# Four graph-attention layers, 32 batches: weights staged all at once, loading over four engines, and orders of their own for the first and last batches

## The chip, the cores and the metric

One core of a Trainium2 chip (trn2). The metric is device time of one execution in microseconds (us), the median of three runs. Every output is float32.

## The reference, cut to what matters

`x` is 32 batches of 512 nodes with 256 features, `adj` a 512 x 512 matrix of integers shared by all batches. Four layers follow one another, each of the form `x = x + layer(relu(layernorm(x)))`:

```python
def attention(h, mask, W, a, slope):          # one head
    Wh = h @ W
    e = leaky_relu((Wh @ a1)[:, None] + (Wh @ a2)[None, :], slope)
    return softmax(where(mask, e, -inf), axis=-1) @ Wh

# layer 0: four heads of 64 features, mask adj != 0, elu
# layer 1: out = relu(h @ mlp1_w + mlp1_b)                     256 -> 512
#          out = elu(elu(attention(out, none, W_fc))) + out    512 features, no mask
#          out = relu(out @ mlp2_w + mlp2_b)                   512 -> 256
#          out = relu(elu(elu(attention(out, adj > 0, W_hand))) + out)
# layer 2: mask (adj > 0) or the diagonal, elu
# layer 3: mask adj != 0, relu
```

## The kernel before, in words

**Arithmetic.** Projections and MLPs are done in three passes on split numbers (`mm3`, L397): each operand has a rounded part "hi" and the rest "lo", and hi x hi, hi x lo, lo x hi are summed. So each of the seven weights (W0, WM1, WFC, WM2, WHA, W2, W3) is held as hi and lo, and each weight of an attention layer has extra columns with its product with `a`. An attention layer transposes normalised x on TensorE (`turn`, L406), makes hi (ScalarE) and lo (VectorE), projects (`project`), takes scores, spreads a row of them over the partitions with transposes (`row`, L440), makes the weights P of 128 x 512 on VectorE from that row and the mask (`weigh`, L646), and multiplies by P (`attend`, L450, 257 columns; layer 0 at L489, 65 columns per head; the unmasked one of layer 1 at L526). The first MLP's result is split into hi on ScalarE (L917) and lo on GpSimd (L1031).

**Lanes.** Batch b runs in lane b % 3, which has its own SBUF buffers (`R`, `Z`, `hT`, `hws`, `rowt` ...) and its own ring of two or three of the eight PSUM banks; x has four slots. Batches in different lanes overlap, two of the same lane don't.

**Order.** `tensor_batch`, `vector_batch`, `scalar_batch` and `pool_batch` are generators: each writes out one batch's instructions for one engine and yields after every step (112 steps on TensorE, 154 on VectorE, 108 on ScalarE, 8 on GpSimd). `in_turns` (L82) lays them out by a string `TURNS` (L66) for each engine. In period t, digit c takes one step of batch t - c, and "w" one step of the loading. The same string serves all 35 periods; digits of batches that don't exist do nothing. So TensorE's 27 steps with digit 0 are layer 0 of the youngest batch, the 51 with digit 1 the wide part of layer 1 and the begin of its second attention, the 34 with digit 2 the rest.

**Loading.** SyncE (SP) fetches x0, x1, x2, then each weight into the same pair of buffers `halves` (parts of lane 2's `R`), one after another (`sync_loads`, L242): it waits for the last weight's subtraction (`s_wlo`) and transposes (`s_wT`). ScalarE makes hi (L319), VectorE lo (L295); for a weight with `a`, TensorE transposes each block of 128 rows (L338), VectorE copies the result (L304), TensorE multiplies by `a` (L345), VectorE writes the extra columns (L307, L309). W0 is loaded ahead of everything, then adj, in two halves, into the same buffers: VectorE makes the 0/1 rows (L358), TensorE transposes them (L392), VectorE copies them into masks of bytes in sixteen pieces (L367). The other weights are loaded by the "w" steps. Batches 1 and 2 wait ahead of their first normalisation on VectorE until all of it is done:

```python
            if b in (1, 2):
                w.wait_ge(s_wAl, 24)
                w.wait_ge(s_wlo, K_BEFORE[7])
                w.wait_ge(s_wT, 12)
                w.wait_ge(s_mT, 16)
```

Of the kernel before, what the change touches and what calls it, by code (L numbers as in the profile page):

```python
# [64 lines left out]

TURNS = {  # L66
    "pe": (
        "ww22112111100w11www1w1w01011220022www0ww22121021w121122w2120121w20w01110ww1ww1102www210102020w20w11w"
        "0w20120101121w10w20w001101w1w211122w212w121121w1"),
    "dve": (  # L70
        "ww2w1w22111w122w21www102w2wwww0002w22ww2w2w22w0ww02w121w222w21w2210ww10w21www2w00022022ww00210022222"
        "001ww0211w221w10w1112ww2221w110w1221w1200211w1w0110w20w0w1121w11212210w120000011w122w00w22w0001w02w1"
        "w022w111122222"),
    "act": (
        "222211221211122212001211010122100121211220w12212221w222121111w1111122101112ww1122112102121122011w210"
        "11211211211122"),
    "pool": (
        "11w1w1w1222"),
}

def in_turns(batch, turns, loading):  # L82
    going, loads = {}, loading()
    for t in range(B + LANES):
        for c in turns:
            if c == "w":
                next(loads, None)
                continue
            b = t - int(c)
            if 0 <= b < B:  # L90
                if b not in going:
                    going[b] = batch(b)
                next(going[b], None)
    for left in [loads] + list(going.values()):
        for _ in left:
            pass
# [14 lines left out]
def build(nc, x_d, adj_d, L0_W, L0_a, m1_w, m1_b, m2_w, m2_b, fc_w, fc_a, ha_w, ha_a, L2_W, L2_a, L3_W, L3_a, out_d):  # L111
    ctx = ExitStack()
    with ctx:
# [18 lines left out]
        def weights(name, kb, fo, nq):  # L132
# [42 lines left out]
        s_zero, s_const, s_id, s_bias = (new_sem(n) for n in ("zero", "const", "ident", "bias"))  # L175
        s_wl = [new_sem(f"wl{c}") for c in range(2)]
        s_al, s_az, s_whi, s_wlo, s_wT, s_wTe, s_wA, s_wAl = (new_sem(n) for n in (
            "al", "az", "whi", "wlo", "wT", "wTe", "wA", "wAl"))
        s_mrow, s_mT, s_mTe, s_mask = (new_sem(n) for n in ("mrow", "mT", "mTe", "mask"))
# [23 lines left out]
        def freed(b, name, i=0):  # L203

            ring = RINGS[b % LANES]
            n = b // LANES * len(USES) + USE_AT[name, i] - len(ring)
            if n < 0:
                return (s_wAl, 24) if b % LANES == 2 else (s_id, 1)
            _, _, kind, k = USES[n % len(USES)]
            return at(kind, n // len(USES) * LANES + b % LANES, *k)  # L210
# [6 lines left out]
        halves = [R[2][:, 0:2, :], R[2][:, 2:4, :]]  # L217
        wT = Z[1][:, 0:512]
        a_st = Z[1][:, 1056:1088].rearrange("p (k q) -> p k q", q=8)
        id_st = Z[2][:, 0:128]  # L220
        mrow = {"ne": R[1][:, 0:2, :], "gt": R[1][:, 2:4, :]}

        LOADS = [(W0, L0_W, "heads", (0,)), (WM1, m1_w, None, (0,)), (WFC, fc_w, fc_a, (0, 1)), (WM2, m2_w, None, (0,)),
                 (WHA, ha_w, ha_a, (0,)), (W2, L2_W, L2_a, (0,)), (W3, L3_W, L3_a, (0,))]
        KB = [w["kb"] for w, _, _, _ in LOADS]

        K_BEFORE = [sum(KB[:n]) for n in range(8)]
        QK_BEFORE = [sum(w["kb"] for w, _, a, _ in LOADS[:n] if a is not None) for n in range(8)]
        Q_BEFORE = [sum(1 for _, _, a, _ in LOADS[:n] if a is not None) for n in range(8)]
        AL_BEFORE = [sum(8 if isinstance(a, str) else 2 for _, _, a, _ in LOADS[:n] if a is not None) for n in range(8)]  # L230

        def wl_count(n, c):
            return sum(1 for _, _, _, cs in LOADS[:n + 1] if c in cs) + (1 if n > 0 else 0)

        def stage(n):

            w, _, _, cs = LOADS[n]
            per = 1024 // w["fo"]
            return [halves[k // per].rearrange("p a n -> p (a n)")[:, k % per * w["fo"]:(k % per + 1) * w["fo"]]
                    for k in range(w["kb"])]  # L240

        def sync_loads(e, w):  # L242
            for n, (wt, w_d, a_d, cs) in enumerate(LOADS):
                fo, kb = wt["fo"], wt["kb"]
                per = 1024 // fo
                wv = w_d.rearrange("(k p) n -> p k n", p=128)
                for c in cs:
                    k0, k1 = c * per, min(kb, (c + 1) * per)
                    if n == 0:
                        w.wait_ge(s_id, 1)  # L250
                    elif n == 1:
                        w.wait_ge(s_mT, 16)
                    else:
                        w.wait_ge(s_wlo, K_BEFORE[n])
                        w.wait_ge(s_wT, QK_BEFORE[n])
                    dst = halves[c].rearrange("p a n -> p (a n)")[:, 0:(k1 - k0) * fo].rearrange("p (k n) -> p k n", n=fo)
                    e.dma_start(dst, wv[:, k0:k1, :]).then_inc(s_wl[c], 16)
                if a_d is not None:
                    w.wait_ge(s_az, Q_BEFORE[n] + 1)
                    if isinstance(a_d, str):  # L260
                        for h in range(4):
                            for t in range(2):
                                p0 = (h % 2) * 64
                                e.dma_start(a_st[p0:p0 + 64, h // 2, t * 4 + h:t * 4 + h + 1],
                                            L0_a[h, t * 64:(t + 1) * 64].rearrange("(p o) -> p o", o=1),
                                            allow_slow_non_contiguous=True).then_inc(s_al, 16)
                    else:
                        ob = fo // 128
                        for t in range(2):
                            e.dma_start(a_st[:, 0:ob, t],  # L270
                                        a_d[t * ob * 128:(t + 1) * ob * 128, 0].rearrange("(k p) -> p k", p=128),
                                        allow_slow_non_contiguous=True).then_inc(s_al, 16)
                if n == 0:
                    for half in range(2):
                        if half == 0:
                            w.wait_ge(s_wlo, 2)
                            w.wait_ge(s_wT, 2)
                        e.dma_start(halves[half].bitcast(I32), adj_v[:, 2 * half:2 * half + 2, :]).then_inc(s_wl[half], 16)
                    e.dma_start(b1[:, :], m1_b.rearrange("(k p) -> p k", p=128),
                                allow_slow_non_contiguous=True).then_inc(s_bias, 16)  # L280
                    e.dma_start(b2[:, :], m2_b.rearrange("(k p) -> p k", p=128),
                                allow_slow_non_contiguous=True).then_inc(s_bias, 16)

        def vector_load(e, w, n):
            wt, _, a_d, cs = LOADS[n]
            tiles, kb, fo, nq = stage(n), wt["kb"], wt["fo"], wt["nq"]
            if a_d is not None:
                if n:
                    w.wait_ge(s_wA, QK_BEFORE[n])
# [849 lines left out]
```

## Time and profile before

| what | value |
|---|---|
| median of three runs | 3269.46 us (3267.59 to 3269.56) |
| profiled execution | 3268.22 us, span 3266.4 us |
| TensorE (PE) busy | 3148.4 us, 96% |
| VectorE (DVE) busy | 2689.4 us, 82% |
| ScalarE (ACT) busy | 1864.1 us, 57% |
| GpSimd (POOL) busy | 326.2 us, 10% |
| mean granted clock of TensorE | 0.982 |

### The profile page before, as it was taken

To read this page: it belongs to the slowest core of one execution; us is meant where nothing else is said; L and a number is where in the kernel's file an instruction comes from. 1 tells how busy PE (TensorE), PEld (TensorE's weight loads), DVE (VectorE), ACT (ScalarE), POOL (GpSimd) and SP (SyncE) were. 2 spreads that over 40 slices of the span, in tenths; PEclk is the share of its full clock that TensorE was granted. 3 is DMA by queue.
4 is the path that set the end of the run, shared out by engine and by line. 5 is a ranking of instruction groups with operands and counts; after the bars stand their busy time and mean duration, and the time that the engine had idled before them with its cause. 6 is when DMAs were issued, how large, how long until landed. Compare 5 with 4: busy or idle time off the path is not lost.

```text
span 3266.4 us, 55502 instructions
## 1 busy us (share of the span) xinstructions
PE 3148.4 (96%) x20480; PEld 2860.2 (88%) x20480; DVE 2689.4 (82%) x7611; ACT 1864.1 (57%) x4627; POOL 326.2 (10%) x265
## 2 busy tenths in 40 slices
PE   5899999999999999999999999999999999999996
PEld 4888899889889888889988889988989988989985
DVE  5578888888888888888888888888888888888865
ACT  1355556565655565655565655655655655655653
POOL 0011100111100111110111110111110111110010
PEclk7799999999999999999999999999999999999997
DMA  2000000000000000000000000000000000000000
GB/s 65 14 1 14 14 14 1 14 14 14 14 14 1 14 14 14 14 14 1 14 14 14 14 14 3 12 14 14 14 14 8 7 14 14 14 14 7 1 7 13
DMA packets 16332, 41.32 MB, mean 13 GB/s; under 512 B 5312, under 2 KB 6848, under 8 KB 16064
## 3 DMA queue, kind: packets, MB, share of 16 engines
q1 hardware_dynamic: 16064, 37.77, 3.3%
q8 instruction: 165, 2.70, 0.3%
q14 instruction: 103, 0.84, 0.1%
HBM read 20.99 MB, written 16.78 MB: 12 GB/s over the span
## 4 chain that ended last, share of the span: by engine, by line
PE 88%; POOL 4%; ACT 4%; DVE 2%; issue 1%; DMA 1%; SPq 0%; POOLq 0%; ACTq 0%; DVEq 0%
PE bank L399 30%; PE bank L457 20%; PE bank L526 14%; PE bank L489 14%; POOL oTlo L1031 4%; PE bank L445 3%; PE bank L413 3%; PE bank L538 2%; ACT O L915 1%; ACT oThi L917 1%; PE bank L435 1%; PE bank L563 1%; ACT Z L978 0%; PE bank L345 0%; DVE x L846 0%
## 5 line engine op out<-in xcount | busy, mean ns | idle before, releaser
L457 PE MATMUL bank<-hw,R 128*128 128x257 f32 x3072 | 735.9, 383 | 6.2 <-ACT Z L983 3.2
L457 PEld LDWEIGHTS bank<-hw,R 128*128 128x128 f32 x3072 | 566.9, 190 | 108.1 <-issue 24.6
L489 PEld LDWEIGHTS bank<-hw,R 128*128 128x128 f32 x4096 | 515.5, 196 | 17.1 <-issue 7.4
L489 PE MATMUL bank<-hw,R 128*128 128x65 f32 x4096 | 515.0, 274 | 7.3 <-DVE R L653 7.3
L526 PE MATMUL bank<-hw,R 128*128 128x257 f32 (+1 forms) x2048 | 492.9, 380 | 0.0
L653 DVE SCALAR_TENSOR_TENSOR R<-bank,E,mask_ne 128x512 f32<-128x512 f32 x640 | 452.6, 742 | 1.4 <-PE bank L445 1.2
L1024 POOL TENSOR_TENSOR rs<-ve,mhalf 128x4 f32<-128x4 f32 x128 | 145.8, 1139 | 2683.0 <-DVE ve L600 2683.0
L526 PEld LDWEIGHTS bank<-hw,R 128*128 128x128 f32 x2048 | 372.6, 189 | 46.1
L399 PE MATMUL bank<-wfc_hi,oThi 128*128 128x256 f32 (+1 forms) x1024 | 303.3, 296 | 30.6 <-POOL oTlo L1031 29.4
L874 ACT COPY Z<-bank 128x258 f32<-128x258 f32 (+1 forms) x640 | 239.0, 374 | 161.6 <-PE bank L399 157.4
L399 PE MATMUL bank<-wfc_lo,oThi 128*128 128x256 f32 (+1 forms) x1024 | 289.4, 283 | 0.0
L399 PE MATMUL bank<-wfc_hi,oTlo 128*128 128x256 f32 (+1 forms) x1024 | 288.1, 281 | 0.0
L888 ACT ACTIVATE hw<-Z,hw 128x256 f32<-128x256 f32 x512 | 241.9, 504 | 2.1
L399 PEld LDWEIGHTS bank<-wfc_hi,oThi 128*128 128x128 f32 x1024 | 193.7, 189 | 43.8 <-POOL oTlo L1031 43.8
L593 DVE BATCH_NORM_STATS2 st<-x 128x6 f32<-128x256 f32 x512 | 215.8, 422 | 9.9
L945 ACT ACTIVATE Z<-bank,rD 128x256 f32<-128x256 f32 x256 | 121.2, 474 | 160.6 <-PE bank L526 134.3
L1031 POOL TENSOR_TENSOR oTlo<-O,oThi 128x512 fp32r<-128x512 f32 x128 | 179.6, 1423 | 228.3 <-ACT oThi L917 225.7
L399 PEld LDWEIGHTS bank<-wfc_hi,oTlo 128*128 128x128 f32 x1024 | 194.3, 190 | 0.0
L399 PEld LDWEIGHTS bank<-wfc_lo,oThi 128*128 128x128 f32 x1024 | 194.0, 189 | 0.0
L621 DVE TENSOR_SCALAR Z<-x,mv,rs 128x256 f32<-128x256 f32 x512 | 178.2, 407 | 6.7 <-POOL rs L1024 3.4
L1001 ACT ACTIVATE Z<-bank,rD 128x256 f32<-128x256 f32 x128 | 60.6, 473 | 213.0 <-DVE rD L662 213.0
L413 PE MATMUL bank<-identr,Z 128*128 128x128 f32 x1024 | 148.4, 281 | 17.1 <-DVE Z L621 17.1
(199 smaller groups left out, 6828.4 us busy)
## 6 DMA issues: line engine op xcount, KB each, us to landing
x<-in_x_dram SPq DMA_DIRECT2D x32, 512.0 KB, 3.2
out_dram<-x SPq DMA_DIRECT2D x32, 512.0 KB, 2.6
R<-in_adj_dram SPq DMA_DIRECT2D x2, 512.0 KB, 4.5
R<-in_L_gnn_mlp_w_dram SPq DMA_DIRECT2D x2, 512.0 KB, 3.9
R<-in_L_gnn_W_fc_dram SPq DMA_DIRECT2D x2, 512.0 KB, 4.2
R<-in_L_gnn_W_dram SPq DMA_DIRECT2D x3, 256.0 KB, 4.0
R<-in_L_gnn_W_hand_dram SPq DMA_DIRECT2D x1, 256.0 KB, 2.6
Z<-in_L_gnn_a_dram SPq DMA_DIRECT2D x8, 0.2 KB, 3.5
```

Of the source, the lines that this page charges most:

```text
L399: i = e.matmul(out, u, v, start=first and q == 0, stop=last and q == 2, skip_group_check=not group)
L413: i = e.transpose(bk[:, n * 128:(n + 1) * 128], hn[:, n, k * 128:(k + 1) * 128], ident[:, :])
L457: ins = e.matmul(bk[:, 0:257], P[:, j, i * 128:(i + 1) * 128], hw[:, j, 0:257], start=(j == 0), stop=(j == NBLK - 1))
L489: ins = e.matmul(bk[:, i * 66:i * 66 + 65], P[:, (4 * h + j) % PTILES, i * 128:(i + 1) * 128], hv[:, j, h, 0:65], start=(j == 0 and i == 0 ...
L526: ins = e.matmul(bank_of(b, "attf", q)[:, 0:n], P[:, j, i * 128:(i + 1) * 128], hw[:, j, c0:c0 + n], start=(j == 0), stop=(j == NBLK - 1))
L593: e.bn_stats(m["st"][:, n, :], xs[b % XSLOTS][:, n, :]).then_inc(up("stat", b))
L621: e.tensor_scalar(hn[:, n, :], x[:, n, :], m["mv"][:, n, 0:1], m["rs"][:, n:n + 1], ALU.subtract, ALU.mult).then_inc(up("hn", b))
L653: e.scalar_tensor_tensor(P[:, t, :], bank_of(b, "row", p)[:, :], m["E"][:, 1, h, j:j + 1], mask[:, j, :], ALU.max, ALU.mult).then_inc(up(" ...
L874: e.copy(raw[s][:, i, 0:n], bank_of(b, f"h{l}", i)[:, 0:n]).then_inc(up("raw", b))
L888: e.activation(hw[:, n, 0:256], raw[s][:, n, 0:256], ACT.Copy, scale=hw[:, n, 256:257]).then_inc(up("hw", b))
L1024: e.tensor_tensor(m["rs"][:, :], m["ve"][:, :], mhalf[:, :], ALU.pow).then_inc(up("rs", b))
L1031: e.tensor_tensor(oT["lo"][:, fo, :], O1[:, fo, :], f32(oT["hi"][:, fo, :]), ALU.subtract).then_inc(up("o1lo", b))
```

## The change

`TURNS` now has three strings for each engine and one set for SP: one for batches 0 to 2 up to the point where batch 3 starts, with the "w" of the loading in it, one cycle for periods 3 to 27, and one for the last batches, in which digit c is batch 31 - c. SP's stores and loads of x are steps too (`sync_batch`). The cycle has the same numbers of steps as before, in another order; TensorE's begins

```
before, "w" left out: 2211211110011110101122002202212102112112221201212001110111022101...
after:                2211211110011110011122002202212112111201212110221212011010012020...
```

In TensorE's last string batch 30's last step has 8 steps behind it (36 in the old layout), and batch 31 begins layer 1 with 132 steps left in all (117). The new string of TensorE for the start begins

```
wwww00ww00000000w00000001000001w000w00w1w111www00w1w0000ww0000w11000101...
```

Every weight has a buffer of its own that later lanes or slots don't need yet:

```diff
-        halves = [R[2][:, 0:2, :], R[2][:, 2:4, :]]
-        wT = Z[1][:, 0:512]
-        mrow = {"ne": R[1][:, 0:2, :], "gt": R[1][:, 2:4, :]}
...
+        x3 = xs[3].rearrange("p b f -> p (b f)")
+        id_st, wT, a_flat = x3[:, 512:640], rowt[1], x3[:, 640:676]
+        adj_st = R[0][:, 0:4, :].bitcast(I32)
+        mrow = {"ne": R[1][:, 0:4, :], "gt": R[2][:, 0:4, :]}
+        tiles0 = [R[1][:, 4, :], Z[2][:, 0:1024], hws[2].rearrange("p b n -> p (b n)")[:, 0:2048], Z[2][:, 1056:2080],
+                  R[2][:, 4, :], rowt[2], x3[:, 0:512]]
...
+        GROUPS = [(0, (0, 1))] + [(2, (k,)) for k in range(4)] + [(n, (0, 1)) for n in (4, 5, 6)]
```

SP issues all of it without a wait but one (for the zeros that `a` of W0 is written into):

```diff
         def sync_loads(e, w):
...
+            e.dma_start(xs[0][:, :, :], x_v[0]).then_inc(xin[0], 16)
+            load_weights(e, 0)
+            for half in range(2):
+                e.dma_start(adj_st[:, 2 * half:2 * half + 2, :], adj_v[:, 2 * half:2 * half + 2, :]).then_inc(s_adj[half], 16)
+            load_scores(e, w, 0)
+            e.dma_start(xs[1][:, :, :], x_v[1]).then_inc(xin[1], 16)
+            load_weights(e, 1)
...
+            load_weights(e, 2)
+            load_scores(e, w, 2)
+            e.dma_start(xs[2][:, :, :], x_v[2]).then_inc(xin[2], 16)
+            load_weights(e, 3)
+            for n in (4, 5, 6):
+                load_weights(e, n)
+                load_scores(e, w, n)
```

The loading is spread: ScalarE makes hi, copies the transposed weights and two of each mask's four blocks (now 128 x 512 at a time); VectorE does the other two, the 0/1 rows, the extra columns and W0's lo; GpSimd makes every other lo:

```diff
+        def gpsimd_lo(e, w, n):
+            wt = LOADS[n][0]
+            for k in range(wt["kb"]):
+                w.wait_ge(s_whi, K_BEFORE[n] + k + 1)
+                e.tensor_tensor(wt["lo"][:, k, 0:wt["fo"]], staged[n][:, k, :], f32(wt["hi"][:, k, 0:wt["fo"]]),
+                                ALU.subtract).then_inc(s_wlo)
+                yield
+
+        def gpsimd_loads(e, w):
+            yield from power(e, w, 0, 0)
+            yield from gpsimd_lo(e, w, 1)
+            yield from power(e, w, 1, 0)
+            yield from gpsimd_lo(e, w, 2)
+            yield from power(e, w, 2, 0)
+            for n in range(3, 7):
+                yield from gpsimd_lo(e, w, n)
```

The wait of batches 1 and 2 for everything is replaced by waits for the buffer that each place overwrites:

```diff
-            if b in (1, 2):
-                w.wait_ge(s_wAl, 24)
-                w.wait_ge(s_wlo, K_BEFORE[7])
-                w.wait_ge(s_wT, 12)
-                w.wait_ge(s_mT, 16)
+            if b == 2:
+                w.wait_ge(s_whi, K_BEFORE[4])
+                w.wait_ge(s_wlo, K_BEFORE[4] - 2)
...
+            if b == 0:
+                w.wait_ge(s_mrow, 4)
+            elif b == 1:
+                w.wait_ge(s_mT, 4)
+                w.wait_ge(s_empty, 1)
+                w.wait_ge(s_wlo0, 2)
+                w.wait_ge(s_wT, 1)
```

and the load of x3 waits for the weights staged in its slot:

```diff
+        def sync_batch(e, w, b):
+            n = b + LANES
+            if n < B:
+                if n >= XSLOTS:
+                    w.wait_ge(xout[n % XSLOTS], 16 * (n // XSLOTS))
+                else:
+                    w.wait_ge(s_id, 1)
+                    w.wait_ge(s_wlo, K_BEFORE[7] - 2)
+                    w.wait_ge(s_wA, 8)
+                e.dma_start(xs[n % XSLOTS][:, :, :], x_v[n]).then_inc(xin[n % XSLOTS], 16)
+            yield
+            w.wait_ge(*at("x3", b, 3, 1))
+            e.dma_start(o_v[b], xs[b % XSLOTS][:, :, :]).then_inc(xout[b % XSLOTS], 16)
+            yield
```

SP's last steps are, in order, the stores of batches 26 and 27, the load of x31, and the stores of 30, 29, 28 and 31.

## Rows read from the trace of the kernel before

**Rows 1.** the page, part 2, granted clock in 40 slices of the span

```profile
PEclk7799999999999999999999999999999999999997
```

**Rows 2.** windows: busy us of PE, PEld, DVE, ACT, POOL; clock; DMA share, GB/s

```profile
1000.00:1500.00 500.00, 494.75 (x3254) 450.27 (x3253) 426.02 (x1203) 295.31 (x735) 51.08 (x40) 1.00 0.03 12
```

**Rows 3.** waits of PE from 1000 to 2000 us: total, times, longest

```profile
PE bank L399 <- POOL oTlo L1031: 9.2, 18, 0.8
```

**Rows 4.** timeline of SP's output stores: start us, us (last row: four stores)

```profile
285.68 0.36 SPq L1054 DMA_DIRECT2D out_dram<-x  x1
...
3015.05 248.59 SPq L1054 DMA_DIRECT2D out_dram<-x  x4
```

**Rows 5.** chain of waits, pieces at full clock late in the run: start, us

```profile
3063.94 5.25 PE bank L526 x24
...
3070.03 0.88 PE bank L413 x8
...
3081.80 0.72 PE bank L399 x6
...
3089.61 2.81 PE bank L399 x12
...
3093.69 2.63 PE bank L489 x24
```

**Rows 6.** timeline of the start: start us, us, engine line operation [idle before]

```profile
8.31 0.71 ACT L319 CAST w_hi<-R 128x256 fp32r<-128x256 f32 x2 [6.30 <-DMA R<-in_L_gnn_W_dram]
...
9.80 0.66 PE L338 MATMUL bank<-identr,R 128*128 128x128 f32 x2 [9.80 <-DMA Z<-in_L_gnn_a_dram]
...
24.63 1.91 PE L413 MATMUL bank<-identr,Z 128*128 128x128 f32 x8
...
46.23 1.94 PE L489 MATMUL bank<-hw,R 128*128 128x65 f32 x8 [7.26 <-DVE R L653]
...
109.06 2.29 PE L413 MATMUL bank<-identr,Z 128*128 128x128 f32 x8 [2.06 <-DVE Z L621]
```

**Rows 7.** windows of 20 us in the start

```profile
60.00:80.00 20.00, 16.65 (x77) 16.09 (x78) 8.53 (x26) 2.77 (x8) 0.00 (x0) 0.50 0.14 39
...
80.00:100.00 20.00, 19.57 (x93) 19.08 (x92) 10.61 (x35) 3.21 (x9) 0.00 (x0) 0.50 0.10 27
```

**Rows 8.** timeline of the start, VectorE

```profile
39.35 1.42 DVE L685 TENSOR_TENSOR hw<-Z,hw 128x256 f32<-128x256 f32 x4
...
74.63 0.74 DVE L653 SCALAR_TENSOR_TENSOR R<-bank,E,mask_ne 128x512 f32<-128x512 f32 x1
...
101.14 0.42 DVE L707 SCALAR_TENSOR_TENSOR x<-Z,x 128x256 f32<-128x256 f32 x1
...
108.59 1.38 DVE L621 TENSOR_SCALAR Z<-x,mv,rs 128x256 f32<-128x256 f32 x4 [1.12 <-POOL rs L1024]
```

**Rows 9.** chain of waits from 0 to 400 us, one piece

```profile
83.63 5.22 PE bank L489 x24
```

**Rows 10.** windows of 1 and 2 us around two falls of the clock

```profile
41.00:42.00 1.00, 0.00 (x0) 0.00 (x0) 1.00 (x1) 0.00 (x0) 0.00 (x0) 0.54 0.95 358
...
181.00:183.00 2.00, 0.62 (x4) 0.41 (x4) 1.26 (x7) 1.39 (x5) 0.00 (x0) 1.00 0.00 0
...
185.00:187.00 2.00, 2.00 (x6) 1.63 (x6) 0.49 (x1) 0.00 (x0) 0.00 (x0) 0.50 0.00 0
```

**Rows 11.** instructions of a line and a tile: ns, min/median/max

```profile
L1031 POOL TENSOR_TENSOR oTlo<-O,oThi x128: 1268/1456/1542, 116.4 to 3125.2; 128x512 fp32r<-128x512 f32 x128
...
L793 DVE SCALAR_TENSOR_TENSOR x<-Z,x x128: 424/425/1398, 194.2 to 3209.0; 128x256 f32<-128x256 f32 x128
```

**Rows 12.** timeline of PE in the last stretch

```profile
3114.56 1.59 PE L413 MATMUL bank<-identr,Z 128*128 128x128 f32 x8
...
3179.03 0.40 PE L399 MATMUL bank<-oThi,wm_lo 128*128 128x512 f32 x1
...
3211.96 2.21 PE L413 MATMUL bank<-identr,Z 128*128 128x128 f32 x8 [9.88 <-DVE Z L621]
```

More of the change, by code:

```diff
@@ L79, with go @@
+    "pool": (
+        ("wwwwww0ww0000wwwwwwwwww1w1111000"),
+        ("11111222"),
+        ("4444455533333444222223313111122000001100120"),
+    ),
+    "sp": (
+        ("001"),
+        ("21"),
+        ("05441312230"),
+    ),
 }
+FIRST, ENDS = 3, 4
 def in_turns(batch, turns, loading):
     going, loads = {}, loading()
[L84 to L93, printed above, removed]
+    def go(b):
+        if 0 <= b < B:
+            if b not in going:
+                going[b] = batch(b)
+            next(going[b], None)
+    start, cycle, end = turns
+    for c in start:
+        if c == "w":
+            next(loads, None)
+        else:
+            go(int(c))
+    for t in range(FIRST, B - ENDS):
+        for c in cycle:
+            go(t - int(c))
+    for c in end:
+        go(B - 1 - int(c))
@@ L225, in build @@
[L225 to L233, printed above, removed]
@@ new lines, in vector_rows, with vector_masks @@
+        def vector_rows(e, w, k):
+            op = ALU.not_equal if k == "ne" else ALU.is_gt
+            for half in range(2):
+                cols = slice(2 * half, 2 * half + 2)
+                w.wait_ge(s_adj[half], 16)
+                e.tensor_scalar(mrow[k][:, cols, :], adj_st[:, cols, :], 0.0, None, op).then_inc(s_mrow)
+                yield
+        def vector_masks(e, w, k):
+            first = 0 if k == "ne" else 4
+            for j in (1, 3):
+                w.wait_ge(s_mT, first + j + 1)
+                e.tensor_copy(maskT[k][:, j, :], bank[7][:, :]).then_inc(s_mEv)
+                yield
@@ L644, in scores, with weigh @@
                 yield
-            def weigh(p, l, h, mask):
+            def weigh(p, l, h, kind):
+                mask = maskT[kind]
+                if kind == "self":
+                    w.wait_ge(s_self, 5)
+                else:
+                    w.wait_ge(s_mEa, 2 if kind == "ne" else 4)
+                    w.wait_ge(s_mEv, 2 if kind == "ne" else 4)
                 w.wait_ge(*at("E", b, l, 1))
@@ L1109, in _ @@
                             channel_multiplier=1).then_inc(s_const)
-            def loading():
-                for b in range(LANES):
-                    yield from power(e, w, b, 0)
-            in_turns(lambda b: pool_batch(e, w, b), TURNS["pool"], loading)
+            in_turns(lambda b: pool_batch(e, w, b), TURNS["pool"], lambda: gpsimd_loads(e, w))
 _INS = ["x", "adj", "L0_gnn_W", "L0_gnn_a", "L1_gnn_mlp1_w", "L1_gnn_mlp1_b", "L1_gnn_mlp2_w", "L1_gnn_mlp2_b",
```

444 lines of the change are left out of this document (238 added, 206 removed).

## Prediction

> **What bounds the kernel now.** I read the page first. TensorE (PE) is busy 96% of the span, VectorE (DVE) 82%, and of the forty slices of granted clock only the first two, 163 us, show less than full [rows 1]. So the middle of the run and its edges have to be read apart. In a 500 us stretch of the middle PE is busy 494.75 us [rows 2]: 1.0 us idle in each batch of 97.5 us, nearly all of it one wait, for POOL's last "lo" of layer 1 (18 times in 1000 us, 9.2 us) [rows 3]. The rhythm is in the output stores: batch 0 leaves at 285.68, batch 28 at 3015.05, so 97.48 us a batch; the last at 3263.6, 248.6 us later [rows 4].
>
> What do the edges cost? I summed PE's written order step by step, each step at the spacing that its kind shows at full clock (in matmul records: 24 of 257 columns 5.25 us, 24 of 65 columns 2.63, 12 of 512 columns 2.81, 6 of 258 columns 0.72, 8 transposes 0.88) [rows 5]. A batch comes to 94 us: 20 for layer 0 (27 steps), 39 for the wide part of layer 1, 35 for the rest. When batch 3 starts, batch 0 is done, batch 1 has had 78 steps (66 us) and batch 2 layer 0 (20): 180 us, plus some 10 for loading. The kernel takes about 281 us (batch 0 is out at 285.7, and its first transposes of layer 1 come at 109.06, three steps into a period). The end, from the start of batch 28 (about 281 + 25 x 97.5 = 2718) to 3266, holds 478 us of steps, 496 at the middle's rhythm, and takes 548. So some 90 us are lost ahead of the middle, 50 behind it.
>
> The first edge, in order. a's small DMAs let PE start at 9.80; batch 0's first transposes come at 24.63; its first layer-0 attention matmul at 46.23, after 7.26 us of idleness; layer 1 starts at 109.06 [rows 6]. Between those last two PE is mostly 83 to 98% busy and still slow: the clock is at 0.50, the lower of its two levels, 1.2 GHz, from 60 to 100 [rows 7]. 24 records of 65 columns take 5.22 us there and 2.63 at the full clock [rows 5, 9]. The clock fell at about 41, in the idle stretch; at 185 it was down after two us in which PE had been busy 0.62 [rows 10]. It isn't full at the very start either, whatever the view says: the eight transposes at 24.63 take 1.91 [rows 6].
>
> **The change, part by part.**
>
> *Staging and order at the start.* Removed: each weight's load waiting for the last one's subtraction and transposes, DVE's sixteen half-width mask copies, twelve copies of turned weights, the batches 1 and 2 held until every weight is ready. Moved: the copies of turned weights and half of the masks to ACT, sixteen weight "lo" subtractions from DVE to POOL (DVE keeps two), x1 and x2 behind adj and a. I walk to four points.
> 1. a for W0 lands as before (the same 1.75 MB ahead, eight issues): 9.8 [rows 6]. Four transposes are done by then; four matmuls 1.0, DVE's two small ops 0.35, four normalisations 1.4 [rows 8]: batch 0's transposes at 12.6, against 24.63.
> 2. From there to the first attention matmul the dependent ops are the same: before, DVE's scaling of hw ended at 40.8, and one weigh op of 0.74 [rows 8] makes 16.9 us after the transposes, with masks in between as now too. Fewer mask copies, one long reduction: I take 13.5. First matmul at 26, not 46.2.
> 3. The attention of layer 0. If PE is at the full clock, DVE sets the pace: 16 weigh ops of 0.74 are 11.9, four closings of 1.6 (three ops of 0.42 [rows 8] and two small) are 6.4, batch 1's normalisation 1.4, then 7 for statistics, POOL's power and normalisation (7.9 from 101.14 to 109.06 before, with other work between) [rows 8]: 27, so layer 1 starts at 53. If PE is at half clock, what its order puts there counts: 16 attention steps of eight records at 0.218 [rows 9] = 28, three rows at 1.1, four WFC groups of four transposes and eight small matmuls, about 0.22 each, 2.7 = 11, batch 1's transposes and two projections 4.4: 47, so at about 74, statistics under the other work. I take half clock: after the projection (around 20) PE has only some twelve transposes until 26, as sparse as the stretches after which the clock fell, and before, it stayed down from 60 to 100 while PE was 83 to 98% busy, mostly with 65-column matmuls [rows 7]. So 74 against 109.06: **35 us**.
> 4. From there to batch 0's store the old kernel takes 176.6 us for 160 us of steps. The new order holds the same plus masks and three groups (5 us at full clock), less batch 1's head start (4): even. PE's idle time after 109 (7 us) and half-clock stretches (some 5) are what a made-to-measure order can recover; I take **3**.
>
> *Bandwidth.* 5.5 MB now go at once on SP's queue, x0 first, W0, adj, a. Before, 1.75 MB were in by 8.31, when ACT could start on W0 [rows 6]; at that rate WFC is in by 17, everything by 25; WFC is needed first at 26. Cost nothing; the cover is layer 0's chain. SP's x3 load now waits for the last subtraction and group; nothing but its own store stands behind it, and batch 3 is wanted after 150.
>
> *POOL.* Six subtractions of 512 columns at 1.46 [rows 11] and ten of 256 columns, between half of that and all of it: 16 to 23 us. They must be ahead of the layer-1 work of batch 0, which is at 74 or later; POOL has nothing else there but four powers. Under half clock: nothing. DVE's cost is the one to look at: an op on two SBUF operands (x of layer 1) takes 0.425 us, but once 1.398 [rows 11], so a DVE op can wait for a POOL op. If every POOL subtraction held DVE for its length, 16 to 23 us. At half clock DVE has 20 us to spare and I take nothing.
> The Trainium skill, "SBUF — State Buffer", section "Who interferes with whom", has a rule that speaks against this part: DVE with two SBUF inputs and a POOL op that reads SBUF exclude each other for the whole instruction. By it the sum would be up to 23 us worse where DVE sets the pace, and the same where PE does; the 1.398 agrees with it.
>
> *End.* In the old order batch 31 enters layer 1 when 99 us of steps are left, and batch 30 ends 30 before the last; then batch 31 is alone: from its second MLP's end (3179.4) to 3266.4 it takes 87 us, with PE idle for 9.88 at one place and its eight transposes behind that at 2.21, the lower clock [rows 12]. The new order puts batch 31 at layer 1 with 110 us of steps left (12 earlier) and keeps batch 30 going to 7 before the end. Batch 31's layer 1 took 64.7 us (3114.56 to 3179.4) around 57 of steps. It now shares with 65: 71.5. So the second MLP ends 12.5 - 6.8 = 6 us earlier. The 87 behind it are one dependent chain; filling gains perhaps 3 of clock, batch 30's steps take 2 of it. SP stores 30, 29 and 28 in that order, all late, ahead of 31: +1 to 2. **6 us**, between 0 and 16.
>
> *The middle.* PE's cycle is nearly the same, and the four matmul steps of layer 1 are still followed by the same two transposes and the projection, so the 1.0 us wait stays. DVE's and ACT's cycles are shuffled more. With 25 cycles, 0.4 us each is 10 us. I see no direction: nothing, from -10 to +15.
>
> **Sum:** 3268.2 (the profiled execution: span 3266.4 and 1.8 around) - 35 - 3 - 6 = 3224. The median of the runs shown is 3269.5, 1.3 more, which is noise here.
>
> **Rivals.**
> - *Full clock through layer 0.* Then 53 in place of 74: 3203, if POOL does not hold DVE; with two thirds of the 23 us 3218. For it: WFC transposes and batch 1's projection are mixed in, and no idle stretch of 7.26 us comes ahead. Against it: such transposes were mixed in from 52 to 100 too, and the clock stayed down [rows 7].
> The Trainium skill, "TensorE: Matmul & The Clock Gate", part 1, says that idleness throttles and sustained activity releases the clock. By it the 98% busy would have brought the full clock before, and would now give 3203; the 0.50 beside it [rows 7] does not agree.
> - *The start gains little,* because one young batch gives PE too little. Layer 1 of batch 0 with only batch 1's layer 0 beside it, a late transfer, POOL between power and "lo": half of the 38 gone, the end at nothing: 3249.
> - *Slower:* the reshuffled cycle. One DVE or ACT step placed after a dependent one makes PE wait in every batch; the 82% of DVE leaves 17 us a batch, so it needs no overload. It decides from 44 / 25 = 1.8 us a batch; at 2.5 us the time is 3287. Against it: PE's order keeps its lags, and both kernels' cycles have the same 154 DVE steps.
> - *The change does nothing:* excluded for the start, where the waits it deletes are in the trace.
>
> **Chances.** Half clock, 3224: 0.5. Full clock, 3203 to 3218: 0.3. Little gain, about 3249: 0.13. Slower: 0.05; same, 0.02. A measurement tells 0.2%, 6.5 us, from no change. The range: below, the full clock with a good end (3203 less 10): 3193; above, the forecast with half of the second rival's 25 and 10 of the cycle's 15: 3246.
>
> **What would show it.** Batch 0's first transposes near 13, first attention near 26, layer 1 near 74 (53) with PE's clock at 0.5 (1.0) from 26; store of batch 0 near 247; 97.5 us between stores in the middle; 2 to 8 us less from batch 27's store to the end. A store interval other than 97.5 by over 0.5 would break the sum, and so would layer 1 of batch 0 beginning after 90.

## The result, and the profile after

The changed kernel takes 3212.99 us (median of four executions, 3203.0 to 3213.97) against 3269.42: 0.9822 of the time before, interval 0.9802 to 0.9842. That is 56.4 us; 3224 was forecast, from 3193 to 3246. The profiled execution took 3213.97 us, its span 3212.2: 54.2 less than the span before.

The page of the changed kernel, parts 1 and 2. PE's busy time fell by 19.6 us, and of the slices of the granted clock only the first is below full, where it was two at the start and the last [rows 1].

```profile
PE 3128.8 (97%) x20480; PEld 2857.5 (89%) x20480; DVE 2638.4 (82%) x7557; ACT 1865.3 (58%) x4639; POOL 333.8 (10%) x281
...
PEclk7999999999999999999999999999999999999999
```

SP's output stores in the timeline (batch 0, batch 25, and the last four as one row), beside [rows 4]. Batch 25's store of the kernel before stands first:

```profile
2722.67 0.34 SPq L1054 DMA_DIRECT2D out_dram<-x  x1
```

```profile
245.03 0.36 SPq L1188 DMA_DIRECT2D out_dram<-x  x1
...
2679.23 0.34 SPq L1188 DMA_DIRECT2D out_dram<-x  x1
...
3203.04 6.39 SPq L1188 DMA_DIRECT2D out_dram<-x  x4
```

The start in the timeline, beside [rows 6, 8]. The first three rows are the loading and batch 0's transposes; then comes POOL's "lo" of WFC beside VectorE's two small operations; then the transposes of E, the first attention matmul, and batch 0's entry to layer 1.

```profile
5.10 1.08 PE L339 MATMUL bank<-identr,R 128*128 128x128 f32 x4 [5.10 <-DMA R<-in_L_gnn_W_dram]
...
11.00 1.85 PE L351 MATMUL bank<-x,rowt 128*128 128x8 f32 x8 [4.82 <-DMA x<-in_L_gnn_a_dram]
...
14.45 1.91 PE L516 MATMUL bank<-identr,Z 128*128 128x128 f32 x8
...
23.07 2.33 POOL L486 TENSOR_TENSOR wfc_lo<-hw,wfc_hi 128x512 fp32r<-128x512 f32 x2
...
23.47 0.90 DVE L748 TENSOR_TENSOR A<-Z,T 128x16 f32<-128x16 f32 x1
...
24.40 1.04 DVE L751 TENSOR_SCALAR A<-A 128x16 f32<-128x16 f32 x1
...
25.92 1.94 PE L548 MATMUL bank<-identr,E 128*128 128x128 f32 x8 [3.22 <-ACT E L1012]
...
28.46 1.94 PE L593 MATMUL bank<-hw,R 128*128 128x65 f32 x8 [0.59 <-DVE R L767]
...
72.93 1.66 PE L516 MATMUL bank<-identr,Z 128*128 128x128 f32 x8
```

Windows (busy us of PE, PEld, DVE, ACT, POOL; then the clock) of the start, the middle and the end. PE is busy for all of 40 to 60, at half clock; in the middle it has 494.08 of 500 us, against 494.75 [rows 2].

```profile
40.00:60.00 20.00, 20.00 (x98) 20.00 (x98) 10.92 (x22) 3.81 (x8) 0.00 (x0) 0.50 0.00 1
60.00:80.00 20.00, 19.32 (x101) 18.51 (x101) 9.78 (x33) 6.22 (x13) 3.42 (x4) 0.67 0.00 0
...
1000.00:1500.00 500.00, 494.08 (x3277) 452.06 (x3276) 419.93 (x1203) 296.88 (x739) 50.56 (x40) 1.00 0.03 12
3140.00:3160.00 20.00, 12.94 (x67) 11.71 (x67) 14.38 (x47) 10.03 (x27) 0.00 (x0) 0.89 0.00 0
3160.00:3180.00 20.00, 14.69 (x69) 12.15 (x70) 12.05 (x34) 8.15 (x23) 1.01 (x1) 0.77 0.00 1
3180.00:3200.00 20.00, 15.71 (x85) 12.36 (x84) 14.26 (x49) 9.65 (x27) 1.01 (x1) 1.00 0.00 1
```

PE's waits from 1000 to 2000 us: the wait for POOL's last "lo" is there as before [rows 3].

```profile
PE bank L502 <- POOL oTlo L1166: 10.5, 20, 0.8
```

PE near the end, beside [rows 12]: the last of batch 31's second MLP, and its next transposes.

```profile
3131.38 0.39 PE L502 MATMUL bank<-oThi,wm_lo 128*128 128x512 f32 x1
...
3161.89 1.36 PE L516 MATMUL bank<-identr,Z 128*128 128x128 f32 x4 [7.31 <-DVE Z L729]
```

With these rows the 54.2 us can be laid out in one line from start to end:

| stretch | before | after | difference | forecast |
|---|---|---|---|---|
| begin to layer 1 of batch 0 | 109.06 | 72.93 | -36.1 | -35 |
| from there to batch 0's store | 176.6 | 172.1 | -4.5 | -3 |
| 25 intervals between stores | 2437.0 | 2434.2 | -2.8 | 0 |
| batch 25's store to the end | 543.7 | 533.0 | -10.8 | -6 |

Two of the signs that the prediction named came out otherwise. From batch 27's store to the end it is 17.8 us less (331.1 for 348.9) and not 2 to 8: the order for the end stores batch 27 itself 7.0 us later against batch 25 (201.9 for 194.9), so this stretch alone doesn't measure the end. And one interval between stores is 98.46, 0.96 from 97.5, where 0.5 was to break the sum; it stands alone, and all 25 together are 2.8 us less.

### The profile page after: what moved, and what is told of

Its sections match the earlier page's. It is cut to its first block, busy times and chain, and to the rows that moved or that the text cites. A ratio compares the mean times of both kernels' runs of the same rounds, so it can differ in the third digit from the quotient of the medians.

```text
span 3212.2 us, 55473 instructions
## 1 busy us (share of the span) xinstructions
PE 3128.8 (97%) x20480; PEld 2857.5 (89%) x20480; DVE 2638.4 (82%) x7557; ACT 1865.3 (58%) x4639; POOL 333.8 (10%) x281
## 4 chain that ended last, share of the span: by engine, by line
PE 81%; DVE 12%; ACT 3%; POOL 2%; issue 2%; SPq 0%; DMA 0%; POOLq 0%; ACTq 0%; DVEq 0%
PE bank L502 28%; PE bank L560 14%; PE bank L593 14%; PE bank L631 14%; PE bank L548 3%; PE bank L516 3%; POOL oTlo L1166 2%; DVE R L767 2%; PE bank L643 2%; DVE Z L729 1%; DVE Z L970 1%; DVE Z L902 1%; DVE x L973 1%; PE bank L538 1%; DVE x L919 1%
## 5 line engine op out<-in xcount | busy, mean ns | idle before, releaser
L593 PE MATMUL bank<-hw,R 128*128 128x65 f32 x4096 | 507.7, 275 | 0.6 <-DVE R L767 0.6
L767 DVE SCALAR_TENSOR_TENSOR R<-bank,E,mask_ne 128x512 f32<-128x512 f32 x640 | 459.0, 740 | 11.9 <-PE bank L548 5.5
L729 DVE TENSOR_SCALAR Z<-x,mv,rs 128x256 f32<-128x256 f32 x512 | 198.6, 431 | 17.2 <-POOL rs L1159 16.8
L1080 ACT ACTIVATE Z<-bank,rD 128x256 f32<-128x256 f32 x256 | 121.3, 474 | 102.5 <-PE bank L631 45.6
L1012 ACT ACTIVATE E<-A,kshift 128x4 f32<-128x4 f32 (+1 forms) x320 | 77.6, 290 | 151.6 <-DVE A L751 148.6
```

The costliest lines, as they stand in the source:

```text
L593: ins = e.matmul(bk[:, i * 66:i * 66 + 65], P[:, (4 * h + j) % PTILES, i * 128:(i + 1) * 128], hv[:, j, h, 0:65], start=(j == 0 and i == 0 ...
L729: e.tensor_scalar(hn[:, n, :], x[:, n, :], m["mv"][:, n, 0:1], m["rs"][:, n:n + 1], ALU.subtract, ALU.mult).then_inc(up("hn", b))
L767: e.scalar_tensor_tensor(P[:, t, :], bank_of(b, "row", p)[:, :], m["E"][:, 1, h, j:j + 1], mask[:, j, :], ALU.max, ALU.mult).then_inc(up(" ...
```

## The experiments

Some kernels below have "spare" matmuls: they read W0 and batch 0's first transposes, write a bank of PSUM that is then overwritten, and nobody reads them. The arithmetic of the result is whole in every kernel.

**Spare matmuls in the idle stretch.** Is the half clock of layer 0 what costs, and does the idleness before it bring it?

```diff
+            def keep(n):
+                if b == 0:
+                    for _ in range(n):
+                        e.matmul(bank[5][:, 0:512], W0["hi"][:, 0, 0:128], hT[0]["hi"][:, 0, :], start=True, stop=True,
+                                 skip_group_check=True)
...
             yield from project(0, hT[s], W0, 0, [at("hTlo", b, 0, k) for k in range(2)])
+            keep(4)
             yield from top(0, 4)
+            keep(12)
             yield from row(0, 0, 0)
...
+                if h == 0:
+                    keep(8)
```

> The changed kernel with 24 spare matmuls of 512 columns (results into a bank that nobody reads), 4 behind batch 0's layer-0 projection, 12 behind the transposes of its maxima, 8 behind the first rows: they fill TensorE's idle stretch between 21.3 and 28.5 us, in which the granted clock fell. It tells why batch 0's attention runs at half clock. Theory A, the idle stretch lets the clock fall and nothing else does: the clock stays at 1.00 from 20 on, layer 1 of batch 0 starts at about 55 in place of 72.9, and the time is some 18 us less, about 3195. Theory B, it falls all the same within a few us of 65-column matmuls: the clock is at 0.50 again by about 35, layer 1 starts at 70 or later, and the time is 3210 to 3214.

3197.51 us (3195.91 to 3200.82), 0.9785 of before (0.977 to 0.9799): 15.5 under the change. In the windows the clock is 1.00 from 20 to 40, through the attention of 65 columns that went at 0.50 before, and falls for a few us near 49; layer 1 of batch 0 begins at 56.44.

```profile
20.00:40.00 20.00, 18.59 (x140) 16.81 (x140) 17.50 (x38) 5.60 (x14) 4.05 (x4) 1.00 0.15 30
...
45.00:50.00 5.00, 4.88 (x38) 4.65 (x37) 4.58 (x15) 2.93 (x7) 0.00 (x0) 0.89 0.00 0
50.00:55.00 5.00, 4.85 (x33) 4.61 (x31) 2.78 (x13) 1.91 (x6) 2.54 (x3) 0.77 0.00 0
```

So 16.5 us of the new start are the clock's, and the attention of 65 columns, met at full clock, went on at 1.00 from 28.44 to 47. That an idle stretch is the only thing that comes ahead of a fall is not shown: near 49 the clock fell to 0.50 for some 3 us while PE was busy 4.88 of 5 us, in batch 1's projection.

**Only the middle twelve.** `keep(4)` and `keep(8)` are left out.

> Of the 24 spare matmuls of 512 columns only the middle 12 are left, between the transposes of tm at 22.1 and the transposes of E, where TensorE is idle for 3.2 us. They do work that nobody reads. Theory A (this one idle stretch takes the clock down at 25 to 26, and once it is down the 65-column matmuls don't bring it back): the granted clock is 1.00 from 25 to 40, layer 1 of batch 0 comes at 56 to 57 and its store at 227 to 228, the time is 3197 to 3199, as with all 24. Rival B (it is the whole thin stretch from 21 to 29.5 that counts, so that half the filling is not enough): the clock falls at 27 to 30, the attention goes at half clock, layer 1 comes at 72 to 73, the store at 245, 3213.

3210.11 us, but from 3195.62 to 3214.15: four executions took 3213.5, 3214.2, 3206.7 and 3195.6. In the profiled one the clock falls at 29 instead of 25.5, after two us (26 to 28) in which PE was busy 0.52, and the attention goes at 0.50 again; its layer 1 begins at 70.58. That is rival B, while the fastest execution has A's time: half the filling leaves it to the execution.

```profile
28.00:30.00 2.00, 2.00 (x16) 2.00 (x16) 2.00 (x5) 0.00 (x0) 0.00 (x0) 0.73 0.00 0
30.00:40.00 10.00, 10.00 (x50) 10.00 (x50) 7.01 (x16) 0.83 (x2) 0.00 (x0) 0.50 0.01 2
```

**What brings the clock back.** Sixteen spare matmuls of 512 columns after the first head, where PE is busy and at half clock; the unchanged new kernel ran beside it.

```diff
             for h in range(4):
...
+                if h == 1:
+                    keep(16)
```

> No spare matmuls in the idle stretch; 16 of 512 columns in the attention of layer 0, after the first head, at about 38, where TensorE is already at half clock and busy. They cost 16 x 0.43 = 7 us at half clock. Theory A (at half clock the 65-column matmuls do not bring the clock back, wider ones do): the granted clock is 1.00 before 50, layer 1 of batch 0 comes at 60 to 68 instead of 72.93, the time is 3203 to 3209. Rival B (the clock stays down for a time that the kind of work does not change): 0.50 until 65 to 70, layer 1 at 80, store at 252, 3220.

> The changed kernel once more, beside the two others. Both theories: 3213 as before, store of batch 0 at 243 to 245.5, and now and then an execution some 10 us faster in which the clock fell later, as one of the four executions so far (3203.0, mean clock 0.993 against 0.990).

With the sixteen: 3205.07 us (3203.29 to 3207.54), 0.9804 (0.9787 to 0.982). The changed kernel itself: 3211.83 (3205.92 to 3212.31), 0.9822. Timeline and windows of the kernel with the sixteen: the clock is back within them, at 39.9, and layer 1 of batch 0 begins at 64.69 (theory A).

```profile
36.34 5.55 PE L581 MATMUL bank<-hT0hi,w_hi 128*128 128x512 f32 x16
```

```profile
35.00:40.00 5.00, 5.00 (x17) 4.24 (x18) 3.47 (x10) 0.84 (x2) 0.00 (x0) 0.52 0.00 0
40.00:45.00 5.00, 5.00 (x40) 4.66 (x38) 1.95 (x3) 0.01 (x1) 0.00 (x0) 1.00 0.00 0
```

But the profiled execution of the unchanged new kernel (3205.92) shows in its windows that the clock can come back without them, here at 45, where it took until nearly 70 in the execution shown above. (Its fall was no later, as the expectation had guessed of such executions; it came back sooner.) So theory A's "do not bring it back" is wrong as a rule; what is left is "later".

```profile
40.00:45.00 5.00, 5.00 (x26) 5.00 (x26) 2.27 (x6) 1.07 (x2) 0.00 (x0) 0.50 0.00 0
45.00:50.00 5.00, 5.00 (x47) 5.00 (x46) 4.93 (x8) 0.83 (x2) 0.00 (x0) 0.99 0.00 0
```

**The same time in narrow ones.** The sixteen are replaced by 32 of 66 columns (`keep(32)` with `[:, 0:66]`).

> As the run with 16 spare matmuls of 512 columns after the first head, but with 32 of 66 columns at the same place: about the same time of TensorE at half clock (32 x 0.22 = 7 us, if they go as the 65-column ones do), a quarter of the columns. The last four executions of the changed kernel already showed that the clock can come back without any wide work: at about 45 in the profiled one (layer 1 at 61.65), at about 65 in the one before. Theory A (wide matmuls bring it back sooner: with the 16 it was back at 39.9 and all four executions took 3203.3 to 3207.5): with narrow ones it stays at 0.50 until 45 to 70, layer 1 at 68 to 80, the median is 3213 to 3220. Rival B (when it comes back is chance, or hangs on the time, and not on the kind of matmul): back at about 40 again, 3203 to 3208.

3218.06 us (3209.77 to 3220.8), 0.9841 (0.9827 to 0.9854). Timeline and windows: 7.01 us of spare work, PE busy for the whole of it, the clock at 0.50 until past 70; layer 1 at 78.19.

```profile
36.03 7.01 PE L581 MATMUL bank<-hT0hi,w_hi 128*128 128x66 f32 x32
```

```profile
35.00:40.00 5.00, 5.00 (x26) 5.00 (x25) 3.47 (x10) 0.83 (x2) 0.00 (x0) 0.50 0.00 0
40.00:45.00 5.00, 5.00 (x25) 5.00 (x25) 0.16 (x1) 0.00 (x0) 0.00 (x0) 0.50 0.00 0
```

At the same place, for about the same time and at the same busy share, wide ones were followed by the full clock in the profiled execution and narrow ones not; the two kernels' times don't overlap. Two limits: each kernel has one profile, and one of the four narrow executions took 3209.77, 8 us under its others, as the unchanged kernel's early returns do, so the difference may be in how often and not in whether. And the wide ones differ in more than columns: the loading of the stationary operand is busy 4.24 of 5 us beside them and 5.00 beside the narrow ones.

**Batch 1 held back.** The string of the start keeps the "w" and batch 0's steps of layer 0 (27 on TensorE, 40 on VectorE, 11 on ScalarE); periods 1 and 2 follow in the cycle's order. So batches 1 and 2 take steps only when the loading is done; staging and spreading stay.

```diff
+def held(k, start, cycle):
+    out, zeros = "", 0
+    for c in start:
+        if c == "w":
+            out += c
+        elif c == "0" and zeros < ZEROS[k]:
+            out, zeros = out + c, zeros + 1
+    return out + "".join(str(t - int(c)) for t in (1, 2) for c in cycle if t >= int(c))
```

> The changed kernel, its staging and its spread loading kept, but the start's order held back: batch 1 starts only when batch 0's layer 0 and all loading steps are written out, then period 1 and period 2 in the changed cycle, as the kernel before had it. It parts the staging from the order of the start. Theory A, my sum: staging and spreading give the most; layer 0's attention with all the loading beside it at half clock ends at about 78 and the two periods behind it take the 176.6 us of before, so batch 0 is stored at 255 to 258 (changed kernel 245.0, before 285.7) and the time is 3223 to 3227. Rival, the early batch 1 and the made-to-measure order give the most: batch 0's store at 270 or later, time 3238 or more.

3235.42 us (3234.51 to 3235.6), 0.9899 (0.9882 to 0.9915): between theory (3223 to 3227) and rival (3238 or more), and nearer the rival. PE's timeline: layer 1 begins at 89.00, and the waits ahead of it (2.40 for the extra columns of WHA, 4.14 for the normalisation) have no work of another batch over them. Batch 0's store leaves at 267.88.

```profile
79.52 1.84 PE L367 MATMUL bank<-x,rowt 128*128 128x2 f32 x8 [2.40 <-DVE wha_lo L442]
...
89.00 2.30 PE L532 MATMUL bank<-identr,Z 128*128 128x128 f32 x8 [4.14 <-DVE Z L745]
```

So of the 40.7 us by which batch 0 leaves earlier, 22.9 need batch 1's early work and its order, and 17.8 are there without. Of the 22.9, 16.1 are there when layer 1 begins; the granted clock of this kernel is 0.50 to 0.59 in each 20 us from 20 to 100, so a part of them is a longer stay at half clock, which this run doesn't separate.

**The end in the cycle's order.**

```diff
+TURNS = {k: (a, c, periods(c, B - ENDS, B + 2)) for k, (a, c, _) in TURNS.items()}
```

`periods` writes the cycle out for the last periods, as the old layout did.

> The changed kernel with the last batches in the cycle's periods again, on all five engines, in place of the orders of their own. Theory A, the order for the end is worth 11 us, as the two profiles have it from batch 25's store on (543.8 against 533.0): 3224. Rival, it is worth only what TensorE's order moves, my 6: 3219. Second rival, the end gains from the reshuffled cycle and not from its own order: 3213.

3224.86 us (3215.96 to 3227.93), 0.9863 (0.9846 to 0.9879): 11.9 over the change, though its four executions lie 12 us apart; in the profiled one batch 25's store to the end takes 546.3 us, 13.3 more than with the change. Windows of its end, and PE's timeline: batch 31 alone, a gap of 9.80 as before [rows 12], the clock at about 0.7 over 60 us.

```profile
3160.00:3180.00 20.00, 8.80 (x39) 7.36 (x37) 11.41 (x36) 6.16 (x14) 1.01 (x1) 0.66 0.00 1
3180.00:3200.00 20.00, 12.60 (x44) 9.77 (x45) 11.46 (x37) 6.01 (x16) 1.01 (x1) 0.72 0.00 0
3200.00:3220.00 20.00, 15.26 (x67) 12.41 (x66) 7.34 (x22) 6.70 (x19) 0.00 (x0) 0.76 0.00 1
```

```profile
3171.00 2.21 PE L524 MATMUL bank<-identr,Z 128*128 128x128 f32 x8 [9.80 <-DVE Z L737]
```

**The old cycle in periods 3 to 27.**

```diff
+TURNS = {k: (a, OLD.get(k, c), z) for k, (a, c, z) in TURNS.items()}
```

`OLD` holds the strings of before for TensorE, VectorE and ScalarE, without "w".

> The changed kernel with the cycle of the kernel before (the loading steps left out) on TensorE, VectorE and ScalarE for periods 3 to 27; start and end keep their new orders. Theory A: the middle's stores come 97.30 us apart in the changed kernel and 97.48 before, so the old cycle costs 25 times 0.18 = 4.5 us: about 3217. Rival, the cycles are the same to within a measurement and the stores' distance has another reason: 3213, stores 97.3 apart.

3215.21 us (3214.44 to 3217.11), 0.9838 (0.9824 to 0.9853). The 2.2 us in the time are within what the runs can tell. The stores tell more: the 25 intervals take 2436.9 us here and 2437.0 in the kernel before, against 2433.8 to 2434.5 in all twelve profiled executions with the new cycle. So the new cycle is worth 2.4 to 3.2 us, under the 4.5 of theory A. One by one they are 97.4 to 97.6 apart here, but for one of 97.90; with the new cycle 97.1 to 97.6, with one pair of 98.46 and 97.80.

**POOL and VectorE.** POOL's first two subtractions of WFC are put behind batch 0's power for layer 1.

```diff
-        ("wwwwww0ww0000wwwwwwwwww1w1111000"),
+        ("wwww0wwww0000wwwwwwwwww1w1111000"),
```

> POOL's two WFC subtractions of 2.33 us (at 23.07) are moved behind batch 0's first power; nothing else is changed. Theory A (POOL on the same port holds the dependent chain ahead of the first attention): VectorE's two 4-column operations at 23.5 and 24.4, 0.90 and 1.04 us beside POOL, go back to 0.17 to 0.18 as in the kernel before, the first attention matmul comes at about 26.9 instead of 28.46, layer 1 of batch 0 at 71.4 instead of 72.93, the store of batch 0 at 243.5 instead of 245.03, the time is 3211.5. Rival B (the subtractions only collide with something else later, the WFC groups wait for them): the first attention at 26.9 too, but TensorE then waits for the subtraction, and the store of batch 0 is at 245 or later, 3213 or more. Rival C (the two operations are slow for another reason): they stay at about 1 us and nothing moves.

3214.03 us (3210.77 to 3215.23), 0.9827 (0.9811 to 0.9843): no gain. Where the subtractions were, theory A is right: the operation takes 0.18 again, and the first attention matmul comes at 27.11. But all four subtractions now run beside batch 0's normalisation for layer 1, and the store leaves at 245.03, to the hundredth as before. Timeline of VectorE, then of POOL:

```profile
23.69 0.18 DVE L748 TENSOR_TENSOR A<-Z,T 128x16 f32<-128x16 f32 x1
...
69.81 2.79 DVE L729 TENSOR_SCALAR Z<-x,mv,rs 128x256 f32<-128x256 f32 x4
```

```profile
67.15 4.65 POOL L486 TENSOR_TENSOR wfc_lo<-hw,wfc_hi 128x512 fp32r<-128x512 f32 x4
```

In the changed kernel POOL was done in time, and the same four normalisations took 1.38:

```profile
68.49 2.33 POOL L486 TENSOR_TENSOR wfc_lo<-hw,wfc_hi 128x512 fp32r<-128x512 f32 x2
...
71.24 1.38 DVE L729 TENSOR_SCALAR Z<-x,mv,rs 128x256 f32<-128x256 f32 x4
```

**Combinations.** First the 24 spare matmuls, the last edit of POOL's order, and 32 spare matmuls ahead of batch 31's transposes for layer 2; then the same with POOL as the change has it; then with twelve more at the start (`keep((8, 0, 6, 6)[h])`).

```diff
+            if b == B - 1:
+                w.wait_ge(*freed(b, "hT2", 0))
+                for _ in range(32):
+                    e.matmul(bank_of(b, "hT2", 0)[:, 0:512], W0["hi"][:, 0, 0:128], hT[s]["hi"][:, 0, :], start=True,
+                             stop=True, skip_group_check=True)
             yield from turn(2)
```

> The 24 spare matmuls of 512 columns at the start, POOL's two WFC subtractions behind the first power, and 32 spare matmuls of 512 columns ahead of batch 31's second set of transposes, where TensorE is idle for 7.3 us and the granted clock is 0.89 and 0.77 in the two stretches of 20 us. They do work that nobody reads. Theory A (the parts add): 3197.5 of the run with spare matmuls, less 1.5 for the port, less 2 to 4 for the end (at 0.77 and 0.89 some 6.8 us of TensorE's time are at half the clock, of which the transposes and matmuls behind the gap are on the chain): 3192 to 3194. Rival B (the end is a dependent chain in which TensorE's clock hardly counts, or the spare matmuls delay the transposes that they precede): end 0 or up to 3 us longer, 3196 to 3200.

> The 24 spare matmuls at the start and the 32 at the end, with POOL's order as the change has it. Theory A (in the last combination the moved subtractions cost 3 us: there the four normalisations of batch 0's layer 1 took 3.94 us beside POOL's four subtractions of WFC, 2.12 in the run with the spare matmuls alone, and the store of batch 0 left 3.1 us later; the end gained 1.3): layer 1 of batch 0 at 56.4, its store at 227.2, 532 us from the store of batch 25 to the end, 3196. Rival B (the 3 us at the start are chance, the end gained nothing): store at 227 to 230, 533.3 us of end, 3197.5 or more.

> The last combination with 12 spare matmuls of 512 columns more, six ahead of each of the last two heads of batch 0's layer 0, where TensorE has gaps of up to 1 us and VectorE sets the pace. Theory A (they fill gaps and the clock does not fall at 48.8): the granted clock is 1.00 through to 60, layer 1 of batch 0 at 55.5, its store at 226, 3193 to 3194. Rival B (the clock falls at 48 to 49 all the same, or the spare matmuls hold up the attention by 12 x 0.23 = 2.8 us): layer 1 at 57 to 59, store at 228 to 230, 3195 to 3198.

With POOL's edit: 3198.51 (3194.98 to 3198.65), 0.978. Without: **3194.98** (3194.49 to 3200.26), 0.9778 (0.9764 to 0.9793), the fastest here, 16.9 under the changed kernel beside it; but 2.5 from the 24 alone (3197.51) is less than the runs can tell. With twelve more: 3197.54 (3194.84 to 3197.87), 0.978. VectorE's and POOL's timelines of the first and the last show why neither got its gain: the normalisations take 3.94 and 3.09 us beside POOL.

```profile
54.46 3.94 DVE L744 TENSOR_SCALAR Z<-x,mv,rs 128x256 f32<-128x256 f32 x4
```

```profile
53.23 4.70 POOL L486 TENSOR_TENSOR wfc_lo<-hw,wfc_hi 128x512 fp32r<-128x512 f32 x4
```

```profile
55.77 3.09 DVE L743 TENSOR_SCALAR Z<-x,mv,rs 128x256 f32<-128x256 f32 x4 [0.22 <-POOL rs L1173]
```

In this window of the last kernel the clock stayed full (0.89 without the twelve). Batch 0's store is at 230.72, not 226 (227.47 without them): the attention ends 1.9 us later, as rival B has it, and the normalisation takes 0.9 us longer (3.09 for 2.23).

```profile
45.00:50.00 5.00, 5.00 (x46) 4.92 (x44) 3.06 (x12) 1.90 (x4) 0.00 (x0) 1.00 0.00 0
```

The 32 at the end are worth 1 to 2 us at most. With them, batch 25's store to the end takes 532.0, 532.1 and 531.0 us in the three kernels; the nine profiled executions with the new order for the end and without them took 533.0 to 534.0 (533.3 with the 24 alone), but for one of 531.8. The clock there did rise, from 0.74 to 0.91 between 3140 and 3160 in the second kernel against the one with the 24 alone:

```profile
3140.00:3160.00 20.00, 12.48 (x58) 10.26 (x59) 12.76 (x35) 7.61 (x21) 1.01 (x1) 0.74 0.00 0
```

```profile
3140.00:3160.00 20.00, 16.58 (x81) 13.07 (x80) 12.64 (x34) 8.22 (x22) 1.01 (x1) 0.91 0.00 1
```

## Why the prediction was right

The forecast's 3224 is 11.0 over the median. By the table above that is 1.1 in step 3's point, 1.5 in the stretch to batch 0's store, 2.8 in the middle and 4.8 at the end; the profiled execution lay 1.0 over the median. All but the end are within what the steps could give.

**The start, steps 1 and 2.** Batch 0's first transposes came at 14.45, not 12.6: `a` landed 1.2 us later than "as before", and eight transposes of the mask's rows stand ahead of them. The first attention matmul came at 28.46, not 26. From one to the other it took 14.0 where 13.5 was taken, and in it are 1.6 us that POOL's subtraction held two small operations (0.90 and 1.04 for 0.18 and 0.17). That POOL costs nothing at half clock was wrong there: VectorE sets the pace of that stretch whatever PE's clock.

**Step 3, half clock.** This was the choice that made the number. Layer 1 began at 72.93 against 74. From the first attention matmul that took 44.5 us, where the step's terms gave 47 (and 26 and 47 are 73; the prediction wrote 74); the clock was back just before 70. That the point is met so closely is luck in part: 2.5 us late at the first matmul and 2.5 short behind it cancel. The rival with the full clock put layer 1 at 53; with spare matmuls holding the clock it came at 56.44, so its sum was sound but for some 3 us. What is shown is that the clock fell in the idle stretch, as the forecast had it; that it stays down through layer 0 is likely, not certain: of eight executions of the changed kernel six took 3211.5 to 3214.0, and two 3203.0 and 3205.9.

**Step 4 and bandwidth.** 172.1 us against 173.6. No wait for the transfer of WFC, WM1 or later weights stands in PE's list of waits up to 250 us (two of 1.2 together are for ScalarE's copies of turned weights); the two transfers waited for are W0 (5.1) and its `a` (4.8). The cost of nothing for 5.5 MB at once held.

**POOL's price.** The subtractions took 1.1 to 1.3 us at 512 columns and 0.64 to 0.78 at 256, some 14 in all against 16 to 23. At full clock the change's own order loses 0.7 on the normalisations (2.12 for 1.38, in the first experiment) and some 1.6 ahead of the attention; with all four of WFC at the normalisations it is 3 us (batch 0's store at 230.28 in the first combination, 227.47 in the second). The rival had two thirds of 23. The Trainium skill, "SBUF — State Buffer", section "Who interferes with whom", gives the lock for two SBUF inputs and lists scalar operations among those that can take the shared pair too; the rows agree with both (TENSOR_TENSOR 0.90 for 0.18, four TENSOR_SCALAR 1.38 to 3.94). The prediction had used the first half alone.

**The end.** The step that was mis-sized. The second MLP of batch 31 ended 4.2 us earlier against batch 25's store (452.2 for 456.4), 6 forecast; the prediction has 110 - 99 = 11 us of earlier entry, wrote 12 and took 12.5, and with 11 its own sum gives 4. The 87 us behind it, taken as one dependent chain, became 80.8: 6.6 less, where 3 of clock less 2 for batch 30's steps and 1 to 2 for SP's order had been given, about nothing. In pieces, from the MLP's end to batch 31's transposes for layer 2 it took 30.5 for 32.9, to those for layer 3 25.6 for 26.9, and to the end 24.7 for 27.5. Two things changed in it: PE's gap before the first of these transposes went from 9.88 to 7.31, and the clock from 0.72 over the last 66 us to 0.91. With the cycle's order at the end both come back (9.80, about 0.7), 11.9 us in all. That run puts back the orders of all five engines, so which of them shortens the chain, and how much of it is the clock, stays open. The prediction could have weighed the clock there more: it reads [rows 1] as below full in the first two slices only, but the last slice is a 7 too.

**The middle** is -2.8 us, well inside -10 to +15, and putting the old cycle back gives the 25 intervals 2.7 us again. It is a small gain of the new cycle, where the prediction took nothing. The rival of a slower cycle needed 1.8 us a batch; it was -0.1.

**What came from what:** by one part undone at a time, 22.4 us are batch 1's early start and the made order, 11.9 the end, about 2 the cycle; the remaining 20 of 56.4 are put down to the staging and the spreading, by subtraction only. They weren't run alone: with each weight waiting for the one before, the new orders don't fit.

## What to carry to other kernels

Look at the granted clock ahead of a dense stretch, not only in it: 7 us of thin work before layer 0 cost 16 us behind it, and 24 matmuls that nobody reads bought them back. When a helper engine's work is moved off a critical place, look what runs beside it at the new one; here 1.5 us gained at the old place were paid again at the new one (four normalisations of 2.79 for 1.38). And give the end of a batched pipeline an order of its own: here it was worth 11.9 us where 6 had been forecast, though the last batch's chain then shared the engines with more work of the one before it.

## What the runs showed of the hardware

- The clock's fall and return are not the same in every execution of one kernel. It fell between 24 and 26 in both profiled executions of the changed kernel and came back at 45 in one and near 70 in the other, with PE busy 1.00 from 30 on until then in both; the times were 3205.9 and 3214.0.
- In one profile each, a busy PE at half clock had the full clock back at 39.9, within sixteen 512-column matmuls, and still had 0.50 past 70 behind 7.01 us of 66-column ones. The Trainium skill, "TensorE: Matmul & The Clock Gate", part 1, has activity release the clock. PE's busy share was 1.00 in both, so by this share alone the return could not be told here.
- A short VectorE operation that meets a POOL subtraction lasted until that ended: 0.90 and 1.04 us for 0.18 and 0.17. Four normalisations of 1.38 in all took 2.12 to 3.94, more with more of POOL's work beside them.
